# Gate logits from fp16 halves, four buffers for attention rows, and a moved cut in a fused attention and expert kernel

## The reference

```python
x = x + attention(layernorm(x), ctx, ctx) @ Wfc.T + bfc     # 32 query heads, 8 key groups
h = layernorm(x)
logits = h @ gate_weight.T                                   # 8 experts
scores = softmax(logits)                                     # top 2 of 8, within 2 of 4 groups
x = x + sum_e(wmat[:, e] * expert_e(h)) + shared(h)          # silu(g) * u, then down
```

## Time and profile before

| | us |
|---|---|
| median of 3 runs | 792.49 |
| lowest, highest | 790.33, 793.11 |
| the profiled execution | 793.74 |
| span inside it | 792.0 |
| TensorE busy | 760.2 (96%) |
| VectorE busy | 576.0 (73%) |
| ScalarE busy | 429.7 (54%) |
| GpSimd busy | 269.5 (34%) |

### The profile page before, as it was taken

How to read it: one execution, slowest core, us unless ns; L and a number is a source line. 1 busy time by engine, 2 the same in 40 slices (tenths; PEclk the granted TensorE clock), 3 DMA queues, 4 the chain that set the end, 5 groups by cost and what they waited for, 6 DMA issues and landing times.

```text
span 792.0 us, 16078 instructions
## 1 busy us (share of the span) xinstructions
PE 760.2 (96%) x5151; PEld 406.6 (51%) x5152; DVE 576.0 (73%) x1194; ACT 429.7 (54%) x843; POOL 269.5 (34%) x224
## 2 busy tenths in 40 slices
PE   6998989999999988999999999999999999999897
PEld 4553533433433334556655656555555555555554
DVE  5767779999999966788789887555555555546767
ACT  3665579999999973455443553434343343323231
POOL 3362007999993301564300101111111111015431
PEclk9999989999999999999999999999999999999999
DMA  9997846556545788898588576877777777569985
GB/s 337 338 391 237 249 145 211 182 162 200 192 122 167 242 323 303 307 333 306 187 226 215 145 172 141 188 175 177 176 177 179 177 185 173 124 164 288 278 238 160
DMA packets 161782, 172.07 MB, mean 217 GB/s; under 512 B 103680, under 2 KB 117504, under 8 KB 161216
## 3 DMA queue, kind: packets, MB, share of 16 engines
q1 hardware_dynamic: 150012, 128.89, 55.8%
q0 software_dynamic: 11120, 41.43, 16.9%
q10 hardware_dynamic: 596, 1.07, 0.4%
HBM read 105.40 MB, written 42.73 MB: 187 GB/s over the span
## 4 chain that ended last, share of the span: by engine, by line
PE 76%; DVE 9%; DMA 7%; ACT 3%; issue 2%; SPq 2%; DVEq 0%; ACTq 0%
PE psum L1465 29%; PE psum L1477 15%; PE psum L1315 8%; PE psum L1301 6%; PE psum L1229 4%; PE psum L1401 4%; PE psum L1205 4%; DMA sb_weights<-attn_dram 3%; PE psum L1332 2%; ACT sb_weights L1025 1%; PE psum L1181 1%; DMA sb_hT<-sb_h 1%; DVE sb_weights L1747 1%; DMA sb_weights<-in_ctxT 1%; DMA sb_weights<-k_parts 1%
## 5 line engine op out<-in xcount | busy, mean ns | idle before, releaser
L1465 PE MATMUL psum<-sb_weights,sb_rows 128*128 (+1 forms) x1608 | 250.8, 313 | 0.6 <-DMA sb_rows<-xnT_dram 0.6
L1465 PEld LDWEIGHTS psum<-sb_weights,sb_rows 128*128 128x128 f16 x1608 | 157.3, 98 | 91.9 <-DMA sb_rows<-xnT_dram 1.1
L1025 ACT ACTIVATE sb_weights<-psum,sb_rows 128x512 f32<-128x512 f32 x256 | 158.6, 684 | 17.2 <-PE psum L1301 15.4
L1697 DVE TENSOR_REDUCE sb_rows<-psum 128x4 f32<-128x1024 f32 x128 | 150.1, 1214 | 6.1 <-PE psum L1229 6.1
L1477 PE MATMUL psum<-sb_weights,sb_hT 128*128 (+1 forms) x630 | 147.4, 379 | 2.5 <-DMA sb_hT<-sb_h 2.5
L894 POOL DMA_INDIRECT sb_rows<-xn_rows,sb_slot_tok x39 | 38.4, 984 | 217.9 <-DVE sb_rows L2286 147.8
L1477 PEld LDWEIGHTS psum<-sb_weights,sb_hT 128*128 128x128 f16 x630 | 61.3, 98 | 68.0 <-DMA sb_hT<-sb_h 3.7
L1301 PE MATMUL psum<-sb_weights 50*128 50x512 f16 x256 | 90.1, 391 | 3.0 <-ACT sb_weights L1025 2.6
L1094 ACT ACTIVATE psum<-psum 128x352 f32<-128x352 f32 x71 | 31.8, 448 | 112.2 <-DVE psum L1947 112.2
L1315 PE MATMUL psum<-sb_weights 128*32 128x256 f32 x1024 | 82.9, 396 | 0.0
L1229 PE MATMUL psum<-sb_weights 48*128 48x256 f16 x512 | 73.1, 275 | 1.2 <-DMA sb_weights<-k_parts 0.6
(11 more groups left out here) (264 smaller groups left out, 1013.1 us busy)
## 6 DMA issues: line engine op xcount, KB each, us to landing
sb_weights<-in_wgu SPq DMA_DIRECT2D x20, 704.0 KB, 7.8
sb_weights<-in_wgu POOLq DMA_DIRECT2D x20, 704.0 KB, 6.2
sb_weights<-in_wdn SPq DMA_DIRECT2D x17, 768.0 KB, 5.6
slot_y<-sb_rows SPq DMA_DIRECT2D x39, 256.0 KB, 2.3
sb_weights<-q_parts SPq DMA_DIRECT2D x96, 64.0 KB, 2.5
x_dram<-sb_rows SPq DMA_DIRECT2D x24, 256.0 KB, 4.4
q_parts<-sb_weights SPq DMA_DIRECT2D x16, 256.0 KB, 4.7
sb_rows<-in_x POOLq DMA_DIRECT2D x16, 256.0 KB, 4.4
```

Of the source, the lines that this page charges most:

```text
L1025: nc.scalar.activation(probs[G % 2][:, kt, pair * 512:(pair + 1) * 512], bank[4 + f % 2], ACT.Exp, scale=exp_scale[:, n:n + 1]).then_inc(e ...
L1465: mm = nc.tensor.matmul(bank[GU_BANKS[par][which]][:, 0:F], x_T[:, xp * D + k * P:xp * D + (k + 1) * P], gu(wp, k, which), start=(k == 0 a ...
L1697: nc.vector.tensor_reduce(to[:, :, j // UB, :, j % UB, qt], psum[:, banks[qt] * 512:(banks[qt] + 2) * 512] .rearrange("p (a h k) -> p a h ...
```

## The change

It does three things. (1) The gate multiplies fp16 halves: gate weights are scaled by a power of two and cut into two fp16 halves (`gw16`), and a gate is four products of the tile's high half with both halves of the weights (16 columns) and four of its low half with the high half (8 columns). The gate weights' maximum goes as an eleventh column through the path that finds the scales of the down weights. The fp32 copy `lnT` is no longer made. Both halves of the logits are evacuated, and softmax_in adds them. gate(t) waits for cut_rows(t). (2) `a_in` has four buffers: the loads of three tiles are issued in unit 13 and the fourth behind the last store of attention rows, and later ones as soon as a buffer was read. SP's loop is written out. (3) cut_rows(15) comes ahead of early_low(0). The diff, cut to its core:

```diff
@@ -206,11 +206,11 @@
...
+        a_in += [dn_tail[:], bfc_sb]
+        TOPS, GW = NE + SH + 1, NE + SH
...
-        lnT = [row(6), row(7)]
-        xb_sb = lnT
+        xb_sb = [row(6), row(7)]
...
         tile_cmp = sb("tile_cmp", [P, (SLOTS + 1) * NE])
+        gw16 = tile_cmp[:, 0:KD * NE].bitcast(F16).rearrange("p (k a e) -> p k a e", k=KD, a=2)
...
@@ -348,7 +351,7 @@
-        a_ld = [sem(f"a_ld{s}") for s in range(2)]
+        a_ld, A_SEEN = (kq_t, kq_all_done, kq_row_done, kq_tt), BLOCKS + 1
...
@@ -527,9 +531,9 @@
                 load_unit((u + 3) // KD, (u + 3) % KD)
                 store_attn(u - 1)
-            def load_attn(b, s):
-
-                sp.dma_start(a_in[s], attn_dram[bass.ds(b * 2 + s, 1)].rearrange("o p d -> (o p) d")).then_inc(a_ld[s], 16)
+            def load_attn(i, r):
+
+                sp.dma_start(a_in[r], attn_dram[i * TPB + r]).then_inc(a_ld[r], 16)
             def load_res_rows(b, s):
                 sp.dma_start(res_in[s], xb_dram[bass.ds(b * 2 + s, 1)].rearrange("o p d -> (o p) d")).then_inc(r_ld[s], 16)
@@ -551,19 +555,20 @@
                     for s in range(2):
                         sp.wait_ge(attn_st[s], FREE + 16 * 2)
                     sp.wait_ge(gu_cut, CUTS_P2)
-                    for s in range(2):
-                        load_attn(0, s)
+                    for r in range(3):
+                        load_attn(0, r)
                 if u == 13:
                     load_ring(5)
                 if u == 14:
                     load_ring(9)
 
-            sp.wait_ge(attn_st[1], FREE + 16 * 2)
+            sp.wait_ge(xb_done, TILES)
+            load_attn(0, 3)
+            sp.wait_ge(attn_st[1], FREE + 16 * BATCH)
+            load_res_rows(0, 1)
             sp.wait_ge(ota_ready, 1)
             load_attn(1, 0)
-            sp.wait_ge(attn_st[1], FREE + 16 * BATCH)
-            load_res_rows(0, 1)
             def tile_of(dram_tiles, t):
                 return dram_tiles[bass.ds(t, 1)].rearrange("o p d -> (o p) d")
@@ -582,27 +587,23 @@
             for t in range(2):
                 sp.wait_ge(ota_ready, t + 2)
-                load_attn((t + 3) // 2, (t + 3) % 2)
+                load_attn(1, t + 1)
                 store_x2(t, t)
                 load_res_rows(1, t)
                 store_xn2(t, t)
-            def token_tile(i, s, more=True):
-
-                if more:
-                    sp.wait_ge(ota_ready, i * 2 + (s + 2))
-                    load_attn(i + (1 + s), 1 - s)
-                store_lnT(i * 2 + s - 2, s)
-                store_x2(i * 2 + s, s)
-                load_res_rows(i + 1, s)
-                store_xn2(i * 2 + s, s)
-
-            LAST_PAIR = TILES // 2 - 2
-            with sp.Fori(1, LAST_PAIR) as i:
-                for s in range(2):
-                    token_tile(i, s)
-            token_tile(LAST_PAIR, 0)
-            token_tile(LAST_PAIR, 1, more=False)
+            def token_tile(t):
+                s = t % 2
+                if t + 5 < TILES:
+                    sp.wait_ge(ota_ready, t + 2)
+                    load_attn((t + 5) // TPB, (t + 5) % TPB)
+                store_lnT(t - 2, s)
+                store_x2(t, s)
+                load_res_rows(t // 2 + 1, s)
+                store_xn2(t, s)
+
+            for t in range(2, TILES - 2):
+                token_tile(t)
             for t in range(TILES - 2, TILES):
                 store_lnT(t - 2, t % 2)
                 store_x2(t, t % 2)
@@ -1037,12 +1038,18 @@
             def lnt_out(t, s, stored):
                 act.wait_ge(lnt_ready, t + 1)
                 act.wait_ge(lnt_stored[s], stored * 16 + FREE)
-                nc.scalar.activation(ln16[s][:, 0:D], bank[4 + s][:], ACT.Copy, scale=X_SCALE)
-                nc.scalar.copy(lnT[s], bank[4 + s][:]).then_inc(lnt_evac, 1)
+                if t >= 2:
+                    act.wait_ge(gate_ready, t - 1)
+                nc.scalar.activation(ln16[s][:, 0:D], bank[4 + s][:], ACT.Copy, scale=X_SCALE).then_inc(lnt_evac, 1)
+
+            def gate_first():
+                act.wait_ge(scale_done, 2)
+                nc.scalar.activation(gw16[:, :, 0, :], gw_sb[:], ACT.Copy, scale=dn_scale[:, GW:GW + 1]).then_inc(gw_high, 1)
             def gate_out(t, s):
                 act.wait_ge(gate_ready, t + 1)
-                nc.scalar.copy(logits[:, bass.ds(t, 1), :], bank[6 + s][:, 0:NE].unsqueeze(1)).then_inc(gate_evac, 1)
+                nc.scalar.activation(route[:, 0:2, t, :], bank[6 + s][:, 0:2 * NE].rearrange("p (a e) -> p a e", a=2), ACT.Copy,
+                                     scale=gate_inv).then_inc(gate_evac, 1)
             def std2(t):
                 act.wait_ge(var_done, t + (BLOCKS + 1))
@@ -1077,7 +1084,7 @@
                 if t - 2 < 2 * HELD:
                     first_part(t - 2)
                 if t == 2:
-                    act.wait_ge(scale_done, 2)
+                    gate_first()
                 if 2 * HELD + 2 <= t < 2 * HELD + 2 + SH:
                     e = NE + t - 2 * HELD - 2
                     dn_first(e, [dn_raw(e % 3)])
@@ -1385,12 +1392,13 @@
-            def ot_transpose(t, s, n):
-                pe.wait_ge(a_ld[s], n * 16 + 16)
+            def ot_transpose(t, r, n):
+                s = r % 2
+                pe.wait_ge(a_ld[r], n * 16 + (16 + A_SEEN))
                 if not (isinstance(t, int) and t < 2):
                     pe.wait_ge(ota_evac, t - 1)
                 for k in range(KD):
-                    tr = nc.tensor.transpose(bank[s][:, k * P:(k + 1) * P], a_in[s][:, k * P:(k + 1) * P], ident[:])
+                    tr = nc.tensor.transpose(bank[s][:, k * P:(k + 1) * P], a_in[r][:, k * P:(k + 1) * P], ident[:])
                 tr.then_inc(ota_ready, 1)
             def out_project(t, s):
@@ -1412,44 +1420,50 @@
                 tr.then_inc(lnt_ready, 1)
             def gate(t, s):
-                pe.wait_ge(lnt_evac, t + 1)
+                pe.wait_ge(ln16_done, t + 1)
                 if not (isinstance(t, int) and t < 2):
                     pe.wait_ge(gate_evac, t - 1)
-                for k in range(KD):
-                    mm = nc.tensor.matmul(bank[6 + s][:, 0:NE], lnT[s][:, k * P:(k + 1) * P], gw_sb[:, k, :],
-                                          start=(k == 0), stop=(k == KD - 1))
+                for part in range(2):
+                    for k in range(KD):
+                        x_k = ln16[s][:, part * D + k * P:part * D + (k + 1) * P]
+                        if part == 0:
+                            mm = nc.tensor.matmul(bank[6 + s][:, 0:2 * NE], x_k, gw16[:, k].rearrange("p a e -> p (a e)"),
+                                                  start=(k == 0), stop=False)
+                        else:
+                            mm = nc.tensor.matmul(bank[6 + s][:, 0:NE], x_k, gw16[:, k, 0, :], start=False, stop=(k == KD - 1))
                 mm.then_inc(gate_ready, 1)
             ot_transpose(0, 0, 0)
...
                 if t == 3:
                     pe.wait_ge(scale_done, 2)
                 ln_transpose(t - 2, t % 2)
-                ot_transpose(t + 1, (t + 1) % 2, (t + 1) // 2)
+                ot_transpose(t + 1, (t + 1) % TPB, (t + 1) // TPB)
                 out_project(t, t % 2)
                 if t == 3:
+                    pe.wait_ge(gw_cut, 1)
                     gate(0, 0)
-            with pe.Fori(2, TILES // 2 - 1) as i:
-                for s in range(2):
-                    ln_transpose(i * 2 + s - 2, s)
-                    ot_transpose(i * 2 + (s + 1), 1 - s, i + (s + 1) // 2)
-                    out_project(i * 2 + s, s)
-                    gate(i * 2 + s - 3, 1 - s)
-            for t in range(TILES - 2, TILES):
+            with pe.Fori(1, BLOCKS - 1) as i:
+                for r in range(TPB):
+                    ln_transpose(i * TPB + (r - 2), r % 2)
+                    ot_transpose(i * TPB + (r + 1), (r + 1) % TPB, i + (r + 1) // TPB)
+                    out_project(i * TPB + r, r % 2)
+                    gate(i * TPB + (r - 3), (r + 1) % 2)
+            for t in range(TILES - TPB, TILES):
                 ln_transpose(t - 2, t % 2)
                 if t + 1 < TILES:
-                    ot_transpose(t + 1, (t + 1) % 2, (t + 1) // 2)
+                    ot_transpose(t + 1, (t + 1) % TPB, (t + 1) // TPB)
                 out_project(t, t % 2)
                 gate(t - 3, (t - 3) % 2)
@@ -1874,6 +1888,9 @@
             dn_abs_max(2 * UG)
             normalise(UNITS * UG - 2)
             dn_abs_max(2 * UG + 1)
+            dve.wait_ge(w_fc, 48)
+            nc.vector.tensor_reduce(dn_max[:, GW:GW + 1], gw_sb[:].rearrange("p k e -> p (k e)"), AX.X, ALU.max,
+                                    apply_absolute_value=True).then_inc(dn_max_done, 1)
 
             def cut_rows(t, s):
...
+            def gate_second():
+                dve.wait_ge(scale_done, 2)
+                nc.vector.tensor_scalar(gate_inv, dn_inv[:, GW:GW + 1], 1.0 / X_SCALE, None, ALU.mult)
```

(40 more changed lines are left out.)

14 lines of the change are left out of this document (7 added, 7 removed).

## The result

Before, the median was 792.21 us (20 runs, 788.32 to 796.36). After, it was **795.44 us** (20 runs, 791.41 to 803.05). The ratio is 1.005, 95% interval 1.0029 to 1.0072. A second set of 12 runs gave 796.29 and 1.0065 (1.0039 to 1.0091), so the loss is real, about half a per cent. Ratios, and the median of experiment 5, leave out the runs that lie over 1.5% above the fastest of their kernel (two in experiment 5, three of the 104 runs of the kernel before).

What follows compares the result with a forecast made beforehand. The prediction took a loop of VectorE, ScalarE and GpSimd, 10.93 us per tile pair, to bound the tile stage, not TensorE. Terms -1.9 + 2.0 + 0.1 + 1.3 = +1.5 us gave 794.0; range 788.0 to 797.5.

Steps and rivals of the forecast that it cites:

- The loop: Token-tile stage: VectorE, ScalarE, GpSimd and back to VectorE take 10.93 us per tile pair, so shorter gates win nothing.
- Rival 2: Token-tile stage: TensorE sets the pace, so shorter gates count, -11.7 us, 780.8; chance 0.17 together with a partial form.
- The tail: End of tile stage: gate(13) waits for cut_rows(13), 2.0 us lost; also 0.1 for softmax_in and 1.3 for a clock fall.
- P(15): Start of residual_norm(15), its addition on VectorE, last tile of the stage; forecast to move by -1.9 us.
- The first wait for rows, P(4) to P(6): Starts of residual_norm(4) to (6): TensorE's 1.37 us wait for attention rows at 331.29 goes, 0.8 us won.
- P(2): Start of residual_norm(2): residual rows come behind one more attention tile in SP's queue, 0.4 us lost, bounds 0 and 0.9.
- gate_second, 0.2 us for its second instruction: VectorE behind residual_norm(2): two small new instructions that cut the gate weights, taken as 0.2 us each, not held by GpSimd.
- rival 1: VectorE behind residual_norm(2): gate_second's second instruction is held by GpSimd's L803, the 1.5 us are gone, 795.5; chance 0.20.
- The sum: Whole kernel: -1.9 + 2.0 + 0.1 + 1.3 = +1.5 us, so the median becomes 794.0.
- the front: First tiles of the stage: residual_norm(2) 0.4 us late, then 1.5 us won up to the start of residual_norm(4).

Runs made afterwards that it cites:

- experiment 5: The change with attention rows back in two buffers (fp16 gates and moved cut_rows(15) kept), against the kernel before: 797.25 us, ratio 1.0056.
- experiment 4: The kernel before with four buffers for attention rows alone, gates and tail untouched: 789.35 us, ratio 0.9963; again 788.08, ratio 0.9954.
- Experiment 1: The changed kernel with gate(13) issued behind the first unit's high half instead of ahead of ln_transpose(14): 792.1 us, ratio 1.0024 to the kernel before.
- experiments 5 and 7: experiment 5, and the changed kernel with both edits but attention rows back in two buffers: the latter 794.69 us, ratio 1.0044 to the kernel before.
- experiment 8: GpSimd's scaling and subtraction of held weight pieces replaced by one memset: in the kernel before 796.42 us, ratio 1.0039; in the kernel after 790.83, ratio 0.9983.
- experiment 2: The changed kernel with gate_second ahead of residual_norm(2) and gate_first ahead of std2(2): 795.55 us, ratio 1.0058 to the kernel before.
- both edits: The changed kernel with gate(13) behind the first unit's high half and gate_second ahead of residual_norm(2): 787.95 us, ratio 0.9963; again 790.98, ratio 0.9984.

## Why the prediction was right, and where it was not

**The loop hides the gate: right.** The steady pairs took 10.92 to 10.98 with either gate (experiment 4), a gate took 0.21 us, and two pairs came down to 9.6 once GpSimd's part was gone. Rival 2 is out.

**The tail: right.** gate(13) waited 4.31 us (forecast some 4.2) and started at P(15) + 2.66 (2.5). The clock fell once there; the transposes and the unit lost 0.46 + 0.97 = 1.4 us (1.3). The token counts moved by 3.3 us against P(15) (3.4). Experiment 1 took the wait and the fall away, and the ratio went from 1.0050 and 1.0065 to 1.0024, some 2 to 3 us.

**The first wait for rows, P(4) to P(6): right in size, too narrow in cause.** It gave 0.77 us (0.8). But experiment 5 has the same 10.94 with two buffers: the shorter gate hides that wait as well. The two parts of the change cover the same waits and don't add.

**P(2), forecast 0.4 us late: wrong.** The rows of one more attention tile, ahead in SP's queue, were priced as a delay; P(0) to P(2) went from 10.06 to 9.08, and VectorE's wait for residual rows from 1.92 to 0.95. The second trace of the kernel after and both traces of four buffers alone had 8.8, but so had the fp16 gates with two buffers (experiments 5 and 7). With fp32 gates and two buffers there are two traces, 10.06 and 9.38 (experiment 8), and only the first waited for residual rows. Most of the gain is thus likely the luck of one transfer.

**gate_second, 0.2 us for its second instruction: wrong, 2.46.** I took L1659, four elements wide and not held, for the nearest row. Against it stood the Trainium skill, page "SBUF — State Buffer", section "Who interferes with whom": a VectorE instruction with two SBUF inputs contends with a GpSimd instruction that reads SBUF, and such contention is an exclusive lock. L1933 (2.46 us beside L804, 0.25 alone, 0.24 beside a memset) and L1950 (2.68 against 1.67) agree with the rule. A held instruction was thus rival 1, and its mechanism came true. Its price did not: 0.57 us (11.50 less the loop's 10.93) and not 1.5. I had P(3) at P(2) + 6.5 and it came at + 6.19; and I had out_project(4) at half clock behind 3.6 us of idle time, where the wait was 2.33 and the granted clock stayed whole.

**The sum.** P(0) to P(15) fell by 2.56 us (forecast 1.9), the tail rose by 3.3 (3.4), so the stage lost 0.74 where I said 1.5. The traces' whole spans differ by 0.4. The medians differ by 3.2 and 4.1, over twice the forecast 1.5. The sum has no term for the 2.5 to 3.4 us between stage and medians, and that the range held the result owes something to its width.

The term in doubt is the front: 0.98 in P(0) to P(2) and 0.94 in P(2) to P(4) were won against a single execution, which had a late transfer and a fall of the clock at 312.6. In experiment 8 the kernel before without GpSimd's part, the same up to that point, waited there 0.36 us for attention rows and not 2.20, and kept its clock. So these gains don't come in every run. But they can't be the whole of it, for they are 1.9 us; and four buffers alone won 3.55 us in the stage against that same execution, and by their ratios 2.9 and 3.6 us in the runs. How often the kernel before has the wait is not shown.

**What stays open.** Beside four buffers alone in the same hour, kernels with fp16 gates are slower by more than their stage shows: experiment 2 by 6.2 us (stage 3.7), experiment 1 by 2.8 (0.3), the kernel after again by 8.2 (4.2), both edits again by 2.9 (-0.3). In the hour between them both edits gave 787.95, 3.8 us under the kernel before, which is the stage's gain (3.84) and leaves nothing over. Part may be the clock: a fall of 3.4 us at half clock takes about 0.002 off the mean (an estimate from 3.4 and 792), and the kernel after has 0.0032 less than the kernel before, one and a half such falls. One is in the tail, in both its traces and in those of experiments 2 and 5. Another, between 731 and 738 us, is in its first trace, behind 2.28 us of waiting for hidden rows, and in those of experiments 2, 5 and the first of 8, and in no other trace. Why it falls there in some was not tried.

With two row buffers and the gates as in the change the ratio is that with four (experiment 5). With both edits it is 1.0044 against 0.9984, 3.7 us in the same hour, though the traces agree to 0.02 us between P(0) and the token counts; the mean clock was 0.9922 against 0.9942. That difference lies outside the stage, and no run here told where.

**The version to keep** is the four buffers alone: 789.35 and 788.08 us, 0.4% under the kernel before, twice. The gates in fp16 add nothing to it that these runs can tell, even with both edits (787.95 and 790.98).

## What to carry to other kernels

An engine that looks full may be waited for by nobody. To see it, take the distance of two starts that waited for nothing, and ask which loop makes it. A consumer moved to a later product (the low half where a copy of the high half did before) also moves everything queued behind it on its engine, and at the edge of a stage that wait cost more than sixteen shorter gates gave. A gain read from one execution's wait for a transfer is unsure, since another execution may not have the wait, and two edits that cover the same wait count once.
